# Four-step recurrence blocks: middle states rebuilt on GpSimd, output products for two places in bursts of eight units, softmax rows side by side in DRAM

## What is computed

```python
q, k, v = layernorm(x) @ Wqkv + b            # 16 heads of 16 channels
y_soft  = softmax(causal(q k^T / 4)) v       # per head, 4096 x 4096
state_t = retention * state_{t-1} + Gamma * (v_t outer k_t / 4)   # per head, 16 x 16
y_stp_t = (W_static + state_t) q_t
alpha   = sigmoid(gelu(layernorm(x) @ gate_w1 + b1) @ gate_w2 + b2)
x1      = x + (alpha * y_soft + (1 - alpha) * y_stp) @ out_w + out_b
out     = x1 + fp8_linear(layernorm(x1))
```

## Time and profile before

| | |
|---|---|
| median of 3 runs | 2063.31 us (2061.59 to 2071.07) |
| the profiled execution's own time | 2065.87 us |
| its span, first to last instruction | 2064.1 us |
| PE busy | 1811.0 us (88%) |
| DVE busy | 1559.0 us (76%) |
| ACT busy | 1384.5 us (67%) |
| GpSimd busy | 1147.8 us (56%) |
| attention stage | from about 250 us to 1892 us |

### The profile page before, as it was taken

How to read it: one execution, slowest core, us unless ns; L and a number is a source line. 1 busy time by engine, 2 the same in 40 slices (tenths; PEclk the granted TensorE clock), 3 DMA queues, 4 the chain that set the end, 5 groups by cost and what they waited for, 6 DMA issues and landing times. The chain is left out here.

```text
span 2064.1 us, 47119 instructions
## 1 busy us (share of the span) xinstructions
PE 1811.0 (88%) x15280; PEld 706.0 (34%) x15280; DVE 1559.0 (76%) x1712; ACT 1384.5 (67%) x2853; POOL 1147.8 (56%) x1130
## 2 busy tenths in 40 slices
PE   5995589999999899999989999999999999986733
PEld 3452123333334333333343333333333333322622
DVE  5433888888888788887888888888888888501867
ACT  2442158888877788888767888887677887864221
POOL 3102266666666566666665675756576767600535
PEclk9996579999999999999999999999999999997865
DMA  4878131223122312322124214122322121102601
GB/s 127 185 186 208 36 91 57 73 60 85 59 64 78 85 58 85 74 77 66 52 74 95 73 55 99 51 63 68 84 70 84 54 62 59 34 6 74 179 7 75
DMA packets 144582, 163.60 MB, mean 79 GB/s; under 512 B 63440, under 2 KB 91088, under 8 KB 144336
## 3 DMA queue, kind: packets, MB, share of 16 engines
q1 hardware_dynamic: 141952, 158.74, 28.6%
q10 hardware_dynamic: 2384, 1.77, 0.3%
HBM read 122.00 MB, written 38.01 MB: 78 GB/s over the span
## 5 line engine op out<-in xcount | busy, mean ns | idle before, releaser
L1327 DVE TENSOR_REDUCE pmax<-PS 128x2 f32<-128x1024 f32 (+3 forms) x1152 | 1251.1, 1131 | 219.7 <-PE PS L1124 185.1
L1277 ACT ACTIVATE probs<-PS 128x512 f32<-128x512 f32 (+3 forms) x2304 | 1126.5, 567 | 321.6 <-PE PS L1158 231.7
L1158 PE MATMUL PS<-Q_st,K_st 50*128 50x512 f16 (+3 forms) x1408 | 414.8, 363 | 30.2 <-ACT probs L1277 13.6
L1042 POOL TENSOR_TENSOR v_exp<-v_exp,k_rows 128x512 f32<-128x512 f32 x256 | 319.9, 1274 | 64.2 <-DMA v_exp<-qkv_t 63.8
L1124 PE MATMUL PS<-K_st,Q_st 48*128 48x512 f16 (+3 forms) x1408 | 349.7, 360 | 5.3 <-DVE pmax L1327 4.8
L1179 PE MATMUL PS<-probs,V_g 128*17 128x512 f32 (+3 forms) x2816 | 342.8, 560 | 0.0
L1158 PE MATMUL PS<-Q_st,K_first 50*128 50x512 f16 (+3 forms) x896 | 275.4, 382 | 20.2 <-issue 7.2
L1124 PE MATMUL PS<-K_first,Q_st 48*128 48x512 f16 (+2 forms) x896 | 239.8, 413 | 52.1 <-DVE pmax L1327 37.1
L1075 POOL TENSOR_TENSOR state<-ends,q_rows 128x516 f32<-128x516 f32 x256 | 276.1, 1111 | 0.0
L1070 POOL COPY carry<-ends 128x4 f32<-128x4 f32 x64 | 12.1, 189 | 469.4 <-DVE ends L1362 469.4
L1158 PEld LDWEIGHTS PS<-Q_st,K_st 50*128 50x128 f16 x1408 | 110.4, 94 | 406.4 <-ACT probs L1277 326.5
(11 more groups left out here) (163 smaller groups left out, 1584.5 us busy)
## 6 DMA issues: line engine op xcount, KB each, us to landing
v_exp<-qkv_t SPq DMA_DIRECT2D x256, 256.0 KB
qkv_t<-proj SPq DMA_DIRECT2D x24, 512.0 KB, 3.7
qk_parts<-parts SPq DMA_DIRECT2D x16, 512.0 KB, 5.3
Q_st<-qk_parts SPq DMA_DIRECT2D x192, 32.0 KB, 3.4
v_rows<-vaug SPq DMA_DIRECT2D x32, 136.0 KB, 6.6
xin<-x SPq DMA_DIRECT2D x8, 512.0 KB, 6.5
k_rows<-qkv_t SPq DMA_DIRECT2D x16, 256.0 KB, 4.0
q_rows<-qkv_t SPq DMA_DIRECT2D x16, 256.0 KB, 5.0
```

The source lines that it names most:

```text
L1042: pool.tensor_tensor(v_exp[:, n % RING], v_exp[:, n % RING], k_rows[:, b % 2], ALU.mult)\
L1158: mm = pe.matmul(PS[:, bank, 0:CH - r * P], keys[rows, pair, kt * P:(kt + 1) * P], Q_st[rows, c, pair, r * P:CH], start=True, stop=(kt < T ...
L1277: act.activation(probs[:, tile % P_SLOTS, h, 0:CH - r * P], PS[:, step[5], 0:CH - r * P], ACT.Exp, scale=SCORE_SCALE).then_inc(exp_done, 1)
L1327: dve.tensor_reduce(pmax[:, s % 2, pair * TPC + j:GH * TPC:PAIRS * TPC, blk], PS[:, bank:bank + SIDES, 0:width], AX.X, ALU.max).then_inc(m ...
```

## The change

- Blocks of four steps stay, but GpSimd rebuilds each block's middle state: `odd` holds end and middle states in turn; the scan writes every second element, and `weigh` fills the others with two more instructions (end state times decay squared, plus the sum of the block's first two steps, still in `pairs`). The states are then two steps apart.
- PE's products are for two places (`PLACES`), 256 columns each. The four column groups now hold two places by two batches, so that one burst handles eight units (`BURST`) and there are 8 in a group in place of 16, in the slots of the odd batches. `state` has four buffers instead of two. The burst's store is 64 rows in one DMA, 32 rows before.
- Only the product at distance 0, for the first of two steps, is left of the inner correction: one `lag` of 256 columns a sweep, one weighting on GpSimd, no sums.
- The scales for even batches (put in by the even slot) move to the U places of the four tiles behind it; those for odd batches stay in the slot beside the burst. All scans keep their slots.
- `y_soft` has the rows of all heads side by side; the last stage reads a chunk with one DMA in place of four, and each partition gets two runs of two rows, not one of four. Weights for places and lags are fewer; two mask tiles are freed after the first stage.

```diff
 def recurrence_steps(last):
     for B in range(N_BATCHES):
         t = period * B + SLOT_AT
-        add(slots, t, "burst", 0, B)
+        if B % 2 == 1:
+            add(slots, t, "burst", 0, B // 2)
         for k in range(BATCH):
             if not (last and B + 2 >= N_BATCHES):
-                add(slots, t, "scale", 0, BATCH * (B + 2) + k)
+                at, when = (slots, t) if B % 2 == 1 else (moves, t + 1 + k)
+                add(at, when, "scale", 0, BATCH * (B + 2) + k)
...
-        for part in range(len(LAG_PARTS)):
-            add(slots, period * (SWEEP_BATCHES * b - 3) + SLOT_AT + LAG_AFTER + part, "lag", 0, b, part)
+        add(slots, period * (SWEEP_BATCHES * b - 3) + SLOT_AT + LAG_AFTER, "lag", 0, b)
...
                     def weigh(g, B):
...
-                        pool.tensor_copy(carry[:, columns(B)], ends[:, B % 2, :, BLOCKS]).then_inc(carried, 1)
-
-                        pool.wait_ge(burst_done, g * N_BATCHES + B + 1)
+                        pool.tensor_copy(carry[:, columns(B)], own[:, :, 2 * BLOCKS]).then_inc(carried, 1)
+                        pool.tensor_tensor(middle, whole,
+                                           decay[:, 1, columns(B)].unsqueeze(2).broadcast_to([P, BATCH, BLOCKS]), ALU.mult)\
+                            .then_inc(middle_scaled, 1)
+                        pool.wait_ge(middle_scaled, n1)
+                        pool.tensor_tensor(middle, middle, pairs[:, B % 2, :, 0:PAIR:2], ALU.add).then_inc(middle_made, 1)
+
+                        pool.wait_ge(burst_done, g * N_BURSTS + B // 2 + 1)
...
-                            pool.tensor_tensor(state[:, B % 2, k].rearrange("p (c e) -> p c e", e=STEP4),
-                                               ends[:, B % 2, k].unsqueeze(2).broadcast_to([P, BLOCKS + 1, STEP4]), q,
+                            pool.tensor_tensor(state[:, B % STATES, k].rearrange("p (c e) -> p c e", e=PLACES),
+                                               own[:, k, 0:PAIR + 1].unsqueeze(2).broadcast_to([P, PAIR + 1, PLACES]), q,
                                                ALU.mult).then_inc(weighed, 1)
...
+                        pe.matmul(PS[:, bank, 0:PAIR], lag_sum[:, b % HALF, :], kq[:, :], start=True, stop=True)\
+                            .then_inc(lag_ready, 1)
+
+                    def burst(g, n, bank):
+                        b, first = n // SWEEP_BURSTS, n % SWEEP_BURSTS * BURST
                         half = b % HALF
...
+                        groups = [(e, q) for e in range(PLACES) for q in range(2)]
...
+                        pe.wait_ge(weighed, g * UNITS + BURST * (n + 1) + 2 * BATCH)
...
                         for k in range(BATCH):
...
+                            for e, q in groups:
+                                own = state[:, (2 * n + q) % STATES, k]
+                                mm = pe.matmul(rows(e, q), sum_e[:, half, first + q * BATCH + k, e, :],
+                                               own[:, 1 + e:1 + e + PLACES * (PAIR - 1) + 1:PLACES],
                                                start=False, stop=(k == BATCH - 1))
...
-                                    act.wait_ge(sums_made, g * (2 * N_BATCHES) + 2 * B)
+                                    act.wait_ge(middle_made, g * N_BATCHES + B)
...
-                            for g in range(NG):
-                                sp.dma_start(soft[:, par, :, g * GH * HD:(g + 1) * GH * HD], soft_rows[g, :, chunk(it, par), :])\
-                                    .then_inc(soft_loaded[par], 16)
+                            sp.dma_start(soft[:, par], soft_rows[:, chunk(it, par)]).then_inc(soft_loaded[par], 16)
```

More of the change, by code:

```diff
@@ L161, in first_steps @@
             steps.append(release)
-            for part in range(len(LAG_PARTS)):
-                steps += [("lag", 0, 0, part, 2), ("lag_evac", 0, 0, part, 2)]
+            steps += [("lag", 0, 0, 2), ("lag_evac", 0, 0, 2)]
         if n == MAXES[s] - 1:
@@ L268, in emptied_before @@
         elif x[0] in ("lag", "lag_evac"):
-            kind, bank, fills, empties = "lag", x[4], x[0] == "lag", x[0] == "lag_evac"
+            kind, bank, fills, empties = "lag", x[3], x[0] == "lag", x[0] == "lag_evac"
         else:
@@ L272, in emptied_before @@
         if fills:
-            found[x[:{"exp": 5, "lag": 4}.get(kind, 3)]] = before.get(bank)
+            found[x[:5] if kind == "exp" else x[:3]] = before.get(bank)
         if empties:
@@ L578, in _ @@
                             k = c1 - 3
-                            for e in range(STEP4):
+                            for e in range(PLACES):
                                 pool.tensor_tensor(
@@ L998, in columns @@
                         return slice(first, first + BATCH)
-                    def by_lag(rows, lag):
-                        steps = rows.rearrange("p (c e) -> p e c", e=STEP4)
-                        return steps[:, 0:LAGS - lag], steps[:, lag:LAGS]
-                    def lag_slots(tile, lag):
-                        at = [n for n, (_, d) in enumerate(LAG_SEGMENTS) if d == lag]
-                        return tile[:, at[0] * BLOCKS:(at[-1] + 1) * BLOCKS].rearrange("p (e c) -> p e c", c=BLOCKS)
@@ L1182, in values @@
                         mm.then_inc(values_done, 1)
-                    def lag(g, b, part, bank):
-                        pe.wait_ge(lag_products, g * (LAGS * N_SWEEPS) + LAGS * b + LAG_PARTS[part][1])
-                        first = LAG_PARTS[part][0]
-                        at = 0
-                        for d in range(first, LAG_PARTS[part][1]):
-                            cols = [n for n, x in enumerate(LAG_SEGMENTS) if x[1] == d]
-                            width = len(cols) * BLOCKS
-                            mm = pe.matmul(PS[:, bank, at:at + width], lag_sum[:, d, b % HALF, :],
-                                           kq[:, cols[0] * BLOCKS:cols[0] * BLOCKS + width], start=True, stop=True)
-                            at += width
-                        mm.then_inc(lag_ready, 1)
```

192 lines of the change are left out of this document (87 added, 105 removed).

## The result

The changed kernel takes 1992.74 us (median of four runs, 1978.54 to 1998.16) where the kernel before took 2067.19 beside it: a ratio of 0.963, 95% interval 0.957 to 0.969. A second series of six runs gave 1986.24 and 0.961 (0.958 to 0.964). The forecast was 2001, with 1950 to 2042 as its range. The profiled execution took 1992.21 us, 73.7 less than that of before.

A forecast was written before the change was run, and what follows sets the result against it. PE was taken to bound the attention stage, with DVE nearly full in plain tiles; gains of 40.9 (31 pairs), 2.5 (last pair), 13.5 (lags) and 5 (last stage) made 62, from 2065.9 to 2003.9, as median 2001 us, range 1950 to 2042.

The forecast's parts named there:

- The stock: Attention stage: each of 64 bursts costs its length on PE, 2.69 us a tile, 172 us to draw on.
- Part 1: Even slot without its burst: costs 1.2 us where it cost 2.69, scan 0.8 and scales 0.4.
- Part 2: Odd slot's burst of eight units, 44 records of 256 columns: 2.8 us, 0.17 more than now, bounds -0.12 and +0.85.
- Part 3: Lags in the groups' walks: each of fifteen gains 0.9 us, 13.5 in all; the first lag gains nothing.
- Part 4: GpSimd's two new instructions, 2.33 us a batch: cost nothing, as over 3 us of its wait for the scan are left.
- Rival B: Scan and GpSimd block each other: the scan held up to 1.29 us more, 32 times, 41 us, 2042 us; chance 0.11.
- Part 5: Last stage, one load of the softmax rows in place of four: gains 5 us, bounds 2 and 9.
- First stage: nothing: First stage: fewer weights lie beside its projections, so it gains nothing.
- A: Rival: all moved work in the attention stage is hidden and the burst takes 2.5; gain 117, 1946 us; chance 0.17.
- C: Rival: moved scan, scales and longer burst are paid in full, 6.89 a pair against 5.38; net +34, 2097 us; chance 0.05.
- D: Rival: no change, Rival B's stalls with the odd slot's burst at 3.5 us, 22 more: 2064 us; chance 0.05.

The follow-up runs named there:

- second trace: The changed kernel run and profiled once more, unedited: 1986.24 us, ratio 0.961 to the kernel before; its profiled execution has a span of 1983.4 us.
- first trace: The changed kernel's first profiled execution, 1992.21 us, laid tile by tile beside that of the kernel before.
- the part by itself: The kernel before with only the softmax rows side by side in DRAM and one load a chunk in place of four: 2061.08 us, ratio 0.9974.
- the first try with moved scans: The changed kernel with eight even scans placed 2 or 3 tiles earlier, six in the groups' walks, two in the last group: 1981.66 us, ratio 0.959.

## Why the prediction was right, point by point

- *The stock.* The burst's tile was 2.7 us longer than a plain one, and 31 even slots gave back 2.72 each: as read.
- *Part 1, the even slot.* Forecast 1.2, found 1.12 (1.03 in the second trace). The split was wrong and its two errors cancelled, which is luck: scales nothing, the scan all of it. Away from the diagonal most slots lie within the scan's bounds of 0.2 and 1.22, and all within 0.0 and 1.31; what I left out are the diagonal tiles, where a late maximum meets a short tile and at times a lower clock, 2.9 to 4.0.
- *Part 2, the odd slot.* Forecast 0.17, found 0.26, so the forecast came out by a false step: "the short record is bound by its weight load and issue, the long one by its columns". The runs showed a short record bound by the step of its moving operand. The 2.8 that I took leaned on the value products' columns, which was nearer to the cause; that the two sizes came out alike (2.62 and 2.85) is two changes that cancel, twice the columns at half the step. The Trainium skill, "TensorE: Matmul & The Clock Gate", Back-to-back issue gap, has 81 ns at 128 columns; here 35 were measured, with four column groups side by side.
- *Part 3, the lags.* 13.7 for 13.5. The first lag, forecast at nothing as "bound by DVE", gave 2.6: at the lower clock, one product in place of three was felt.
- *Part 4, GpSimd.* Nothing, as forecast, and another 2.1 a batch would cost some 7 us. The margin was misread: "over 3 us are left" came from waits of 6.91 and 7.61, but in the same trace the last group has shorter ones beside maxima, 3.97 at the least, from which the same sum leaves next to nothing; 1.25 was left.

```profile
1611.99 0.19 POOL L1070 COPY carry<-ends 128x4 f32<-128x4 f32 x1 [3.97 <-DVE ends L1362]
```

- *Rival B* falls by its size and not by its mechanism: where a scan meets a GpSimd product it waits for it, but they meet at 4 of 64 scans and the median stays 1.223.
- *Part 5.* Last stage 5 forecast: 2.7 in the first trace, 6.2 in the second; the part by itself 5.4 (1.4 to 9.3). "First stage: nothing" is the term that failed: 5.6 us, by the step of the gate products' stationary operand. I had read the diff there as fewer weights on GpSimd and not looked at PE's line.
- *Rivals.* A (all hidden, 1946) falls on the scan, and is right on the scales; C (paid in full) would have wanted 2.7 a pair and 1.4 was paid; D has nothing for it. The chance that lay outside the stated range was 0.19 (C, D and half of A), where the prediction says about 0.17.

The 62 us of the forecast are 12 short of the first trace's 73.7: 8 ahead of the first tile and 5 in tiles and passages that I had not counted, 1 in the slots and lags, less 2 in the last stage.

The 5 in other tiles are 2.9 in the passages between groups and 2.4 elsewhere, and the latter are mostly the clock: in the last group's end the kernel before ran at the lower clock in tiles 122, 123 and 134 to 136 (0.50 to 0.66), the changed one in the last three alone (0.51, 0.64 and 1.00), so that the kernel before lost 3.6 us there, while the changed one lost 1.5 at tiles 37 and 38 of the third walk, at 0.84 and 0.63. Tiles 122 and 123, before and then after:

```profile
1826.00:1834.00 8.00, 7.18 (x28) 1.52 (x28) 0.68 (x2) 4.12 (x9) 0.00 (x0) 0.57 0.00 0
```

```profile
1759.00:1764.00 5.00, 3.98 (x27) 1.03 (x21) 0.68 (x2) 3.67 (x8) 0.00 (x0) 1.00 0.02 3
```

So not all of the 73.7 is owed to the change's work: such spells come and go (below), and one more or one less is up to 10 us, about as much as the forecast was off.

What stays open: the passages between groups, which no run took apart, and what decides on a spell of the lower clock.

## What to carry to other kernels

Read the step of every operand in the rows that you scale from: a duration "per record" is one of a step, too, and a change that halves the step moves it by more than the column count does. Put an indivisible piece of VectorE work right ahead of a short one of the loop it delays, never by a tile that is short itself, and look at the granted clock behind it. Align two traces tile by tile before you explain a difference: with a scatter of 3 to 11 us from loads and clock, medians alone would have called the first try with moved scans a near miss when its walks had gained 12.

## What the runs showed of the hardware

- *The step.* A TensorE record of 128 fp32 columns took 35 ns with its moving operand at a step of 8 bytes and 59 ns at 16 bytes; at 4 bytes there is little more to win (65 to 62 ns at 256 columns). As a stationary operand, four products (eight records) with 128x128 weights took 1.01 us at a step of 8 bytes and 1.93 at 16. The Trainium skill, "SBUF — State Buffer", Door 1: The DMA port swizzle, speaks of 16-byte lines that want two hits or more for full bandwidth; the traces agree, since steps of one and two elements have them and the step of four has one. The same passage gives 4 fp32 as the distance that one can stride for free; as a step of four elements that does not hold here (59 against 35 ns), and the measurement decides.
- *A scan waits out a GpSimd product.* A scan with two inputs in SBUF that started while a GpSimd product was under way ended 1.09 us behind it, however much was left of the product (0.2 to 1.3 us, in 70 of the 71 scans of over 1.3 us in the fourteen traces); by itself it takes 1.22.
- *A spell of the lower clock that comes or not.* In the last group's end PE has no maxima beside it and is busy some 16 of 20 us. Of the twelve traces of the change and its edits, six kept the clock at 1.00 in the window of 20 us that starts 70 before the last value product, and their last group took 372 to 381 us; five (moved scans, scales back, the middle instruction thrice, bursts at steps one and four) had 0.57 to 0.68 there and took 388 to 393; one (the gates' step) had 0.75 and took 383. That is some 10 us with the same instructions in that end. What decides it isn't known: the edits lie far ahead of it, and other edits don't have it.
